# GpSimd makes the output weights' low half, new step lists for both ends, and a last tile whose feed-forward runs in halves

## The chip, the cores and the metric

The kernel runs on one core of a Trainium2 chip. The metric is device time in microseconds. A core has TensorE (PE) for matrix products, VectorE (DVE), ScalarE (ACT) and GpSimd (POOL) for elementwise work, and SyncE (SP), which here only issues DMAs. Each engine works through its own instruction list in order, and waits on semaphores for the others.

## What is computed

```
q  = layernorm(layernorm(x)) @ Wq,  q = q*(1+scale) + shift     # 32 batches of 112 rows, 256 wide, 16 heads of 64
kv = layernorm(ctx) @ Wkv                                       # 32 batches of 375 keys
x  = x + tanh(g_x) * (softmax(q k^T / 8) v @ Wout)
h  = gelu(bitlinear(layernorm(x), W1, b1))                      # 256 -> 1024
x  = x + tanh(g_f) * bitlinear(h, W2, b2)                       # 1024 -> 256
bitlinear(x, W, b): rms-normalise each row, scale by 127/max|row|, round and clip to int8;
                    W ternary (-1, 0, 1) by its mean absolute value; product, rescaled, plus b
```

## The kernel before

Attention goes batch by batch, 0 to 31. Products are made in three float16 matmuls (high times high, high times low, low times high), so each weight and each intermediate is split into a high half (`_h`, made by ACT) and a low half (`_l`, the rest after subtraction, mostly made by DVE). The feed-forward goes by token tiles 0 to 27 of 128 rows; one tile becomes ready after about each batch.

No loop order is left to chance: for each engine there are written lists of named steps. `ORDER` is the steady part, `FIRST` what runs in its place at the start (batches 0 and 1), and `LAST` what runs at the end (batches 30 and 31 and the last tiles). A pair like `("K3", 1)` is step K3 of batch 1. For the steps of tiles, `sequence` turns the number b into tile b - b//8 - 1, so 31, 30, 29, 28, 27 in the lists are the tiles 27, 26, 25, 24, 23. In this document the tile number is given.

The steps that matter here, in the order in which a batch or a tile meets them:
- LNA (POOL) and LNW (ACT): scales and normalised context `ctx_n`, `x_n`, from the statistics BA, BB, BS (DVE). Z0, Z1, ZX (PE): their transposes. ZF, ZXF (ACT), ZS, ZXS (POOL): evacuation and split.
- K0 to K7, V00 to V12, Q0, Q1 (PE): projections, each in one of three PSUM banks (`work`), evacuated by KH or VH (ACT), then KL or VL (DVE); for Q by QF (ACT) and QS (POOL). A bank is given to the jobs in turn, so a job waits for the evacuation of the third job before it.
- S0 to S7 (PE): scores of a pair of heads; M (DVE) the maxima, E (ACT) the exponentials, PH (ACT or DVE) the high half of the probabilities, PL (POOL) the low half, T (SP) the DMA transpose, A0 to A7 (PE) the product with v, N (DVE) the division. S of pair p waits for E of pair p-2, and E of pair p waits for PL of pair p-2.
- OO0, OO1 (PE) with OH (ACT), OT (DVE): transposed attention output. WO (PE): output projection of a tile. X1, XST, SC1 (DVE), RM1, XQ, XB (POOL), XR (ACT): residual, statistics, quantisation of the tile. XT (PE), XTE (DVE): its transpose. F0, F1 (PE), HE0, HE1 (DVE): first linear layer in two halves of 512 columns. GE, SQ, HR (ACT): gelu, sum of squares, rounding. HMX, SC2 (DVE), RM2, HQ (POOL): maximum, scales, quantised hidden row. HT (PE), HTE (DVE): its transpose. F2 (PE), YE (DVE), ST (SP): second layer, output row, store. Up to tile 25 the two transposes are DMA transposes issued by SP (XD, HD); for tiles 26 and 27 (`TAIL = 2`) PE does them.
- At the start the weights come in by DMA and are split: WKH0, WKH1, WQH, WVH, WOH (ACT, `wkv_h` and so on), WKL0, WKL1, WQL, WVL, WOL (DVE). AS0, AS1 (DVE) sum the absolute feed-forward weights.

The line numbers in the profile: 448 PL, 473 and 475 LNA, 510 HQ, 521 the ACT weight splits, 598 and 599 LNW, 608 E, 629 GE, 632 SQ, 637 HR, 650 the DVE weight splits, 662 AS, 805 HTE of the last tiles, 814 HTE of the others, 820 HE, 824 HMX, 718 to 725 the scales, 832 YE, 844 to 846 the three matmuls of a product, 863 S, 918 Z, 946 HT, 965 F2.

Of the kernel before, what the change touches and what calls it, by code (L numbers as in the profile page):

```python
# [1007 lines left out]
```

## Time and profile before

| | us |
|---|---|
| median of 3 runs | 1119.22 (1117.04 to 1120.62) |
| the profiled execution, its own time | 1121.15 |
| its span | 1119.3 |
| PE busy in the span | 1068.0 (95%) |
| ACT busy | 970.7 (87%) |
| DVE busy | 946.4 (85%) |
| POOL busy | 772.1 (69%) |

The busy times say which engine is nearly full; the 40 slices of the page say where it is not, and the chain that ended last says what the end of the span waited for. Waits, the timeline and the stretches then show which instruction ended an idle time.

### The profile page before, as it was taken

The numbers are of one execution on the slowest core, as the hardware profiler recorded it, in microseconds if no ns is written. First come the engines' busy times: TensorE is split into PE (matmuls) and PEld (weight loads), VectorE is DVE, ScalarE is ACT, GpSimd is POOL, SyncE is SP. The second block draws the span as 40 slices with busy tenths as digits, with TensorE's granted clock in tenths as the row PEclk, the third lists the DMA queues.
The fourth block names the chain that finished last, engine by engine and source line by source line (L and its number), as shares of the span: only waits on it lengthen the run. The fifth ranks groups of instructions, "written<-read, shape, count | busy, mean of one in ns | idle before, by whom it ended". The sixth has DMA issues, their size and how long they took to land.

```text
span 1119.3 us, 32134 instructions
## 1 busy us (share of the span) xinstructions
PE 1068.0 (95%) x11910; PEld 733.5 (66%) x11910; DVE 946.4 (85%) x2112; ACT 970.7 (87%) x1865; POOL 772.1 (69%) x837
## 2 busy tenths in 40 slices
...
PEclk9899999999999999999999999999999999999996
...
GB/s 272 86 109 107 101 106 122 123 97 126 115 114 118 133 104 101 123 115 110 134 119 99 120 118 99 122 127 104 115 119 120 109 137 112 97 124 106 112 114 24
DMA packets 408153, 129.08 MB, mean 115 GB/s; under 512 B 389792, under 2 KB 402848, under 8 KB 408000
## 3 DMA queue, kind: packets, MB, share of 16 engines
...
## 4 chain that ended last, share of the span: by engine, by line
PE 78%; ACT 9%; DMA 5%; issue 3%; DVE 2%; POOL 1%; POOLq 0%; DVEq 0%; SPq 0%; ACTq 0%
PE work L844 16%; PE work L846 16%; PE work L845 16%; PE ps_s L863 11%; DMA pt<-pn 4%; PE ps_o L844 3%; PE ps_o L846 3%; PE ps_o L845 3%; PE work L927 3%; ACT prob L608 2%; ACT q_f L574 2%; ACT L608 2%; PE work L956 2%; PE work L918 2%; PE work L965 2%
## 5 line engine op out<-in xcount | busy, mean ns | idle before, releaser
L448 POOL TENSOR_TENSOR pn<-prob,pn 112x750 f16<-112x750 f32 x256 | 400.2, 1569 | 117.5 <-ACT pn L618 97.8
L608 ACT ACTIVATE prob<-ps_s,neg_max 112x375 f32<-112x375 f32 x512 | 265.1, 573 | 10.5 <-DVE neg_max L759 7.5
L759 DVE TENSOR_REDUCE neg_max<-ps_s 112x2 f32<-112x750 f32 x256 | 237.6, 929 | 21.6 <-PE ps_s L863 21.5
L844 PE MATMUL ps_o<-v_h,pt 128*128 128x65 f16 (+1 forms) x1536 | 166.5, 194 | 9.1 <-DMA pt<-pn 7.6
L844 PE MATMUL work<-z,wkv_h 128*128 128x375 f16 x512 | 168.4, 329 | 2.7 <-POOL z L469 2.5
L681 DVE SCALAR_TENSOR_TENSOR k_l<-work,k_h 128x375 f16<-128x375 f32 x256 | 136.4, 541 | 38.4 <-ACT k_h L530 38.3
L530 ACT ACTIVATE k_h<-work 128x375 f16<-128x375 f32 x256 | 121.4, 488 | 53.4 <-PE work L846 48.6
L846 PE MATMUL work<-z,wkv_l 128*128 128x375 f16 x512 | 167.2, 327 | 0.0
L845 PE MATMUL work<-z,wkv_h 128*128 128x375 f16 x512 | 166.8, 326 | 0.0
L845 PE MATMUL ps_o<-v_l,pt 128*128 128x65 f16 (+1 forms) x1536 | 166.3, 192 | 0.0
L846 PE MATMUL ps_o<-v_h,pt 128*128 128x65 f16 (+1 forms) x1536 | 166.3, 193 | 0.0
L844 PEld LDWEIGHTS ps_o<-v_h,pt 128*128 128x128 f16 (+1 forms) x1536 | 143.4, 97 | 22.5 <-DMA pt<-pn 10.4
L845 PEld LDWEIGHTS ps_o<-v_l,pt 128*128 128x128 f16 (+1 forms) x1536 | 142.6, 98 | 9.5
L844 PE MATMUL work<-wkv_h,z 128*128 128x512 f16 (+1 forms) x384 | 146.8, 382 | 1.2 <-DVE k_l L681 1.2
L846 PE MATMUL work<-wkv_h,z 128*128 128x512 f16 (+1 forms) x384 | 145.5, 379 | 0.0
L845 PE MATMUL work<-wkv_l,z 128*128 128x512 f16 (+1 forms) x384 | 145.4, 379 | 0.0
L846 PEld LDWEIGHTS ps_o<-v_h,pt 128*128 128x128 f16 (+1 forms) x1536 | 142.5, 97 | 0.0
L681 DVE SCALAR_TENSOR_TENSOR v_l<-work,v_h 128x512 f16<-128x512 f32 (+1 forms) x192 | 128.3, 681 | 7.1 <-ACT v_h L530 6.6
L530 ACT ACTIVATE v_h<-work 128x512 f16<-128x512 f32 (+1 forms) x192 | 115.3, 601 | 11.4 <-PE work L846 9.5
L618 ACT ACTIVATE pn<-prob 112x750 f16<-112x750 f32 x128 | 107.8, 842 | 0.1
L574 ACT ACTIVATE q_f<-work,side_add,side_mul 128x112 f32<-128x112 f32 x256 | 93.9, 466 | 2.9 <-PE work L846 2.8
L863 PE MATMUL ps_s<-k_h,q_h 64*112 64x375 f16 x512 | 88.7, 343 | 2.2 <-ACT prob L608 1.8
(135 smaller groups left out, 2723.5 us busy)
## 6 DMA issues: line engine op xcount, KB each, us to landing
...
pt<-pn SPq DMA_TRANSPOSE x256, 3.5
...
stage<-in_wkv SPq DMA_DIRECT2D x2, 1024.0 KB, 9.3
stage<-in_w SPq DMA_DIRECT2D x2, 1024.0 KB, 13.1
stage<-in_wq SPq DMA_DIRECT2D x1, 1024.0 KB, 8.2
```

The source lines that it names most:

```text
L448: g.tensor_tensor(buf[:, 1, :, 0:SK], prob[:, p % 2], buf[:, 0, :, 0:SK], ALU.subtract).then_inc(p_lo, 1)
L530: a.activation(dst, src, ACT.Identity, scale=1.0 / W_SCALE).then_inc(hi_done, 1)
L574: i = a.activation(q_f[:, c, :], work[:, BANK[job], m * SQ:(m + 1) * SQ], ACT.Identity, bias=add, scale=mul)
L608: i = a.activation(prob[:, p % 2, h, :], ps_s[0:SQ, 2 * (p % 2) + h, 0:SK], ACT.Exp, bias=neg_max[:, 2 * (p % 2) + h:2 * (p % 2) + h + 1])
L618: a.activation(pn[g % PBUF][:, 0, :, 0:SK], prob[:, p % 2], ACT.Identity).then_inc(p_hi_act, 1)
L681: v.scalar_tensor_tensor(out=dst, in0=src, scalar=1.0 / W_SCALE, in1=hi_part, op0=ALU.mult, op1=ALU.subtract).then_inc(evacuated[BANK[job] ...
L759: v.tensor_reduce(neg_max[:, 2 * (p % 2):2 * (p % 2) + 2], ps_s[0:SQ, 2 * (p % 2):2 * (p % 2) + 2, 0:SK], X, ALU.max, negate=True).then_in ...
L844: t_.matmul(dst, sh, mh, start=(n == 0), stop=False)
L845: t_.matmul(dst, sh, ml, start=False, stop=False)
L846: i = t_.matmul(dst, sl, mh, start=False, stop=(n == len(pairs) - 1))
L863: i = t_.matmul(ps_s[0:SQ, 2 * (p % 2) + h, 0:SK], q[r, p, :], k[r, p, :], start=(n == 0), stop=(n == 2))
L927: i = t_.transpose(w[:, m * SQ:(m + 1) * SQ], attn[:, c * P:(c + 1) * P], ident[0:SQ, 0:SQ])
```

## The change

Five things are changed.
1. The step WOL (low half of the output weights) goes from DVE's list, where it was two SCALAR_TENSOR_TENSOR of 128x1024, to POOL's, where it is one TENSOR_SCALAR and one TENSOR_TENSOR of 128x2048, ahead of PL0 of batch 0.
2. All `FIRST` and `LAST` lists are new orders of the same steps. `ORDER` is as it was.
3. WO waits for the second half of the attention output (OO1) only ahead of its fifth of eight column blocks, rather than ahead of the first.
4. For the last tile (27) GE, HR, HQ, HT, HTE and F2 run in two halves of 512 columns; the first half of HT goes to a free bank of `ps_s`.
5. `deq2t`, the output scale, has two columns, one for even and one for odd tiles.

```diff
 FIRST["ACT"]
-    ("LNW", 0), ("WKH0", 0), ("ZF1", 0), ("ZF0", 0), ("WQH", 0), ("WKH1", 0), ("KH1", 0), ("WVH", 0),
-    ("KH0", 0), ("KH2", 0), ("ZXF", 0), ("WOH", 0), ("KH4", 0), ("KH3", 0), ("LNW", 1), ("QF0", 0),
+    ("WKH0", 0), ("LNW", 0), ("WKH1", 0), ("ZF1", 0), ("ZF0", 0), ("WQH", 0), ("KH0", 0), ("ZXF", 0),
+    ("WVH", 0), ("KH1", 0), ("KH2", 0), ("KH3", 0), ("LNW", 1), ("KH4", 0), ("QF0", 0), ("ZF0", 1),
+    ("KH5", 0), ("KH7", 0), ("ZF1", 1), ("WOH", 0), ("KH6", 0), ("VH02", 0), ("E0", 0), ("KH0", 1),
 FIRST["PE"]
-    ("Z1", 0), ("Z0", 0), ("K1", 0), ("K0", 0), ("K2", 0), ("ZX", 0), ("K4", 0), ("K3", 0),
-    ("Q0", 0), ("Z0", 1), ("K7", 0), ("K5", 0), ("K6", 0), ("Z1", 1), ("S0", 0), ("S1", 0),
+    ("Z1", 0), ("Z0", 0), ("ZX", 0), ("K0", 0), ("K2", 0), ("K1", 0), ("K3", 0), ("K4", 0),
+    ("Q0", 0), ("Z0", 1), ("K5", 0), ("K7", 0), ("Z1", 1), ("S0", 0), ("K6", 0), ("V02", 0),
 FIRST["DVE"]
-    ("BA", 0), ("BB", 0), ("BS", 0), ("WKL0", 0), ("ZS1", 0), ("WQL", 0), ("WKL1", 0), ("KL1", 0),
-    ("BA", 1), ("KL0", 0), ("BB", 1), ("KL2", 0), ("BS", 1), ("WVL", 0), ("KL4", 0), ("KL3", 0),
-    ("WOL", 0), ("KL7", 0), ("KL5", 0), ("AS0", 0), ...
+    ("BA", 0), ("BB", 0), ("BS", 0), ("WKL0", 0), ("WKL1", 0), ("ZS1", 0), ("WQL", 0), ("BA", 1),
+    ("KL0", 0), ("BB", 1), ("BS", 1), ("KL1", 0), ("KL2", 0), ("WVL", 0), ("KL3", 0), ("KL4", 0),
+    ("AS0", 0), ("KL5", 0), ("KL7", 0), ...
 FIRST["POOL"]
+    ("LNA", 0), ("ZS0", 0), ("SD", 0), ("ZXS", 0), ("LNA", 1), ("QS0", 0), ("ZS0", 1), ("ZS1", 1),
+    ("WOL", 0), ("PL0", 0), ("QS1", 0), ("PL1", 0), ("PL2", 0), ("LNA", 2), ("PL3", 0), ("ZXS", 1),
 LAST["PE"], its end
-    ("A2", 31), ("A3", 31), ("WO", 30), ("F2", 28), ("A4", 31), ("A5", 31), ("A6", 31), ("A7", 31),
-    ("XT", 30), ("OO0", 31), ("OO1", 31), ("F0", 30), ("F1", 30), ("WO", 31), ("F2", 29), ("XT", 31),
-    ("F1", 31), ("F0", 31), ("HT", 30), ("F2", 30), ("HT", 31), ("F2", 31),
+    ("S6", 31), ("S7", 31), ("OO1", 30), ("V10", 31), ("F0", 29), ("A2", 31), ("V12", 31), ("A3", 31),
+    ("F1", 29), ("WO", 30), ("A4", 31), ("A5", 31), ("F2", 27), ("OO0", 31), ("A6", 31), ("A7", 31),
+    ("OO1", 31), ("XT", 30), ("F1", 30), ("WO", 31), ("F0", 30), ("F2", 28), ("XT", 31), ("F0", 31),
+    ("F1", 31), ("F2", 29), ("HT", 30), ("F2", 30), ("HT", 31), ("F2", 31),
 LAST["ACT"], its end
-    ("OH0", 31), ("OH1", 31), ("HR", 29), ("GE", 30), ("SQ", 30), ("XR", 31), ("HR", 30), ("GE", 31),
+    ("XR", 30), ("OH1", 31), ("HR", 29), ("GE", 30), ("XR", 31), ("SQ", 30), ("HR", 30), ("GE", 31),
     ("SQ", 31), ("HR", 31),
 LAST["DVE"], its end
-    ("N3", 31), ("XTE", 30), ("SC2", 29), ("OT0", 31), ("OT1", 31), ("HE1", 30), ("HE0", 30), ("X1", 31),
-    ("XST", 31), ("HTE", 29), ("SC1", 31), ("HMX", 30), ("YE", 29), ("XTE", 31), ("SC2", 30), ("HE1", 31),
-    ("HE0", 31), ("HTE", 30), ("YE", 30), ("HMX", 31), ("SC2", 31), ("HTE", 31), ("YE", 31),
+    ("X1", 30), ("XST", 30), ("YE", 27), ("N2", 31), ("OT0", 31), ("SC1", 30), ("N3", 31), ("HMX", 29),
+    ("XTE", 30), ("OT1", 31), ("HTE", 28), ("SC2", 29), ("HE1", 30), ("X1", 31), ("XST", 31), ("HE0", 30),
+    ("SC1", 31), ("YE", 28), ("HMX", 30), ("XTE", 31), ("HTE", 29), ("SC2", 30), ("HE1", 31), ("HE0", 31),
+    ("YE", 29), ("HMX", 31), ("HTE", 30), ("SC2", 31), ("YE", 30), ("HTE", 31), ("YE", 31),
 LAST["POOL"], its end
-    ("PL5", 31), ("XB", 29), ("PL6", 31), ("PL7", 31), ("RM1", 30), ("RM2", 29), ("XQ", 30), ("HQ", 29),
-    ("XB", 30), ("XB", 31), ("RM1", 31), ("RM2", 30), ("XQ", 31), ("HQ", 30), ("RM2", 31), ("HQ", 31),
+    ("PL5", 31), ("HQ", 28), ("PL6", 31), ("PL7", 31), ("RM1", 30), ("XB", 30), ("XQ", 30), ("RM2", 29),
+    ("HQ", 29), ("RM1", 31), ("XQ", 31), ("RM2", 30), ("HQ", 30), ("RM2", 31), ("XB", 31), ("HQ", 31),
 LAST["SP"], its end
-    ("RS", 30), ("T1", 31), ("T2", 31), ("ST", 27), ("XD", 29), ("HD", 28), ("T3", 31), ("T4", 31),
-    ("T5", 31), ("T6", 31), ("T7", 31), ("ST", 28), ("RS", 31), ("HD", 29), ("ST", 29), ("ST", 30),
+    ("T1", 31), ("XD", 29), ("T2", 31), ("T3", 31), ("T4", 31), ("RS", 30), ("T5", 31), ("T6", 31),
+    ("T7", 31), ("RS", 31), ("ST", 27), ("HD", 28), ("HD", 29), ("ST", 28), ("ST", 29), ("ST", 30),
     ("ST", 31),
...
+            def split_output_weights():                       # POOL
+                pool.wait_ge(hi_split[3], 1)
+                g.tensor_scalar(wout_f, wout_f, W_SCALE, 0.0, ALU.mult, ALU.add)
+                pool.drain()
+                g.tensor_tensor(wout_l[:], wout_f, wout_h[:], ALU.subtract).then_inc(lo_split[3], 1)
...
+                        for half in LAST_HALVES:               # GE of the last tile, ACT; LAST_HALVES is [1, 0]
+                            act.wait_ge(evacuated[BANK[f"F{half}", b]], USE[f"F{half}", b])
+                            c = slice(half * HALF, (half + 1) * HALF)
+                            a.activation(hid_g[:, c], hid[:, c], ACT.Gelu).then_inc(gelu_done, 1)
...
+                if name == "HT" and b == NT - 1:               # PE
+                    pe.wait_ge(exp_done, B * PAIRS)
+                    pe.wait_ge(hq_ready, b + 1)
+                    for c in range(4):
+                        i = t_.transpose(ps_s[:, 0, :].bitcast(F16)[:, c * P:(c + 1) * P], hid_q[:, c * P:(c + 1) * P], ident_h[:])
+                    i.then_inc(half_turned, 1)
+                    pe.wait_ge(hq_ready, b + 2)
+                    for c in range(4):
+                        i = t_.transpose(wh[:, c * P:(c + 1) * P], hid_q[:, (c + 4) * P:(c + 5) * P], ident_h[:])
```

## Rows read from the trace of the kernel before

**Rows 1.** The page: busy share, TensorE's granted clock in 40 slices.
```profile
PE 1068.0 (95%) x11910; PEld 733.5 (66%) x11910; DVE 946.4 (85%) x2112; ACT 970.7 (87%) x1865; POOL 772.1 (69%) x837
...
PEclk9899999999999999999999999999999999999996
```

**Rows 2.** Waits of PE over the span: total us, times, longest.
```profile
PE work L918 <- ACT x_n L599: 17.0, 2, 13.3
```

**Rows 3.** Stretches: length, busy us (instructions) PE, PEld, DVE, ACT, POOL, granted clock, DMA, GB/s.
```profile
75.00:1040.00 965.00, 953.29 (x10795) 659.61 (x10794) 836.27 (x1882) 870.63 (x1692) 700.19 (x734) 1.00 0.67 115
...
34.00:35.00 1.00, 1.00 (x5) 0.48 (x4) 0.24 (x1) 0.00 (x0) 0.00 (x0) 0.50 0.32 129
...
36.00:37.00 1.00, 1.00 (x10) 0.72 (x10) 1.00 (x2) 0.15 (x1) 0.00 (x0) 1.00 0.00 0
...
1084.00:1086.00 2.00, 0.99 (x33) 0.89 (x30) 1.68 (x7) 0.00 (x0) 1.21 (x3) 1.00 0.65 114
...
1098.00:1100.00 2.00, 1.13 (x6) 0.35 (x4) 1.74 (x4) 0.55 (x1) 0.41 (x1) 0.50 0.00 0
```

**Rows 4.** Timeline of ACT at the start: start us, us, instruction, [idle before, releaser].
```profile
13.07 1.04 ACT L521 ACTIVATE wkv_h<-stage 128x1024 f16<-128x1024 f32 x1
...
25.64 1.91 ACT L521 ACTIVATE wout_h<-stage 128x2048 f16<-128x2048 f32 x1 [1.66 <-DMA stage<-in_wout]
...
28.19 1.57 ACT L598 ACTIVATE ctx_n<-ctx_in,ln_nb,ln_rs 125x256 f32<-125x256 f32 x3
```

**Rows 5.** Timeline of PE at the start: Z0 of batch 1, first scores.
```profile
30.40 0.86 PE L918 MATMUL work<-ident,ctx_n 125*128 125x125 f32 x3 [3.74 <-ACT x_n L599]
...
36.74 0.37 PE L863 MATMUL ps_s<-k_h,q_h 64*112 64x375 f16 x2
```

**Rows 6.** DMA issues from 1.5 to 1.9 us: first half of wkv, us to landing.
```profile
stage<-in_wkv SPq DMA_DIRECT2D x1, 1024.0 KB, 8.7
```

**Rows 7.** Timeline of DVE at the start: WVL.
```profile
24.66 2.73 DVE L650 SCALAR_TENSOR_TENSOR wkv_l<-stage,wkv_h 128x1024 f16<-128x1024 f32 x2
```

**Rows 8.** Timeline of POOL at the start: LNA of batches 1 and 2, PL0.
```profile
25.13 2.02 POOL L473 TENSOR_TENSOR ln_rs<-ln_ve,minus_half 125x4 f32<-125x4 f32 x1
...
42.25 1.56 POOL L448 TENSOR_TENSOR pn<-prob,pn 112x750 f16<-112x750 f32 x1 [1.64 <-ACT pn L618]
...
49.95 1.02 POOL L473 TENSOR_TENSOR ln_rs<-ln_ve,minus_half 125x4 f32<-125x4 f32 x1 [0.23 <-DVE ln_ve L702]
```

**Rows 9.** Timeline of PE at the end: last attention product, then HT and F2 of tile 27.
```profile
1087.16 0.20 PE L844 MATMUL ps_o<-v_h,pt 128*128 128x65 f16 x1 [0.75 <-DMA pt<-pn]
...
1112.50 1.01 PE L946 MATMUL work<-ident_h,stage 128*128 128x128 f16 x8 [5.30 <-POOL stage L510]
1114.39 1.86 PE L965 MATMUL work<-w_t,stage 128*128 128x256 f16 x8 [0.88 <-DVE stage L805]
```

**Rows 10.** Timeline of DVE at the end: XTE, HTE, YE, HMX.
```profile
1099.60 0.29 DVE L801 TENSOR_SCALAR xqt<-work 128x256 f16<-128x256 f16 x1 [0.16 <-PE work L942]
...
1104.50 0.69 DVE L805 TENSOR_SCALAR stage<-work 128x1024 f16<-128x1024 f16 x1 [1.81 <-PE work L946]
1107.34 0.48 DVE L832 SCALAR_TENSOR_TENSOR y<-work,deq2t,stage 128x256 f32<-128x256 f32 x1 [2.15 <-PE work L965]
1107.74 1.21 DVE L824 TENSOR_REDUCE amax<-stage 128x1 f32<-128x1024 f32 x1
```

**Rows 11.** Timeline of ACT at the end: GE and HR of tile 27.
```profile
1102.72 1.06 ACT L629 ACTIVATE stage<-stage 128x1024 f32<-128x1024 f32 x1 [0.55 <-DVE stage L820]
...
1109.98 1.24 ACT L637 ACTIVATE stage<-stage,round_col,qs 128x1024 f32<-128x1024 f32 x1 [5.02 <-DVE qs L725]
```

**Rows 12.** Timeline of POOL at the end: HQ of tile 24, RM2 and HQ of tile 27.
```profile
1070.45 1.05 POOL L510 TENSOR_SCALAR stage<-stage 128x1024 f16<-128x1024 f32 x1 [3.75 <-ACT stage L637]
...
1105.38 0.54 POOL L507 TENSOR_TENSOR g_rs<-g_ve,minus_half 128x1 f32<-128x1 f32 x1
...
1111.31 1.05 POOL L510 TENSOR_SCALAR stage<-stage 128x1024 f16<-128x1024 f32 x1 [5.39 <-ACT stage L637]
```

More of the change, by code:

```diff
@@ L224 @@
     BANK[job], USE[job] = n % WORK_BANKS, n // WORK_BANKS + 1
+GELU_COUNT = [t + 1 if t < NT - 1 else t + 2 for t in range(NT)]
+LAST_HALVES = [int(s[0][2]) for s in sequence("DVE") if s[0] in ("HE0", "HE1") and s[1] == NT - 1]
 HI_COUNT = {s: n + 1 for n, s in enumerate(s for s in sequence("ACT") if s[0][0:2] in ("KH", "VH"))}
@@ L294, in build @@
         ssq, g_ve, g_rs = (sb(n, [P, 1]) for n in ("ssq", "g_ve", "g_rs"))
-        amax2, clip2, inv2, qs2, deq2, deq2t = (sb(n, [P, 1]) for n in ("amax2", "clip2", "inv2", "qs2", "deq2", "deq2t"))
+        amax2, clip2, inv2, qs2, deq2 = (sb(n, [P, 1]) for n in ("amax2", "clip2", "inv2", "qs2", "deq2"))
+        deq2t = sb("deq2t", [P, 2])
         xqt_r, hqt_r = sb("xqt_r", [P, KC, P], F16), sb("hqt_r", [P, FF // P, P], F16)
@@ L509, in step @@
                     pool.wait_ge(scaled2, b + 1)
-                    g.tensor_scalar(hid_q[:], hid_r[:], -ROUND, 1.0, ALU.add, ALU.mult).then_inc(hq_ready, 1)
+                    if b < NT - 1:
+                        g.tensor_scalar(hid_q[:], hid_r[:], -ROUND, 1.0, ALU.add, ALU.mult).then_inc(hq_ready, 1)
+                    else:
+                        for half in range(2):
+                            pool.wait_ge(scaled2, b + 1 + half)
+                            c = slice(half * HALF, (half + 1) * HALF)
+                            g.tensor_scalar(hid_q[:, c], hid_r[:, c], -ROUND, 1.0, ALU.add, ALU.mult).then_inc(hq_ready, 1)
             for name, b in sequence("POOL"):
@@ L624, in step @@
                         act.wait_ge(tern_ready[1], 1)
-                    for half in range(2):
-                        act.wait_ge(evacuated[BANK[f"F{half}", b]], USE[f"F{half}", b])
                     if b > 0:
                         act.wait_ge(scaled2, b)
-                    a.activation(hid_g[:], hid[:], ACT.Gelu).then_inc(gelu_done, 1)
+                    if b < NT - 1:
+                        for half in range(2):
+                            act.wait_ge(evacuated[BANK[f"F{half}", b]], USE[f"F{half}", b])
+                        a.activation(hid_g[:], hid[:], ACT.Gelu).then_inc(gelu_done, 1)
+                    else:
+                        for half in LAST_HALVES:
+                            act.wait_ge(evacuated[BANK[f"F{half}", b]], USE[f"F{half}", b])
+                            c = slice(half * HALF, (half + 1) * HALF)
+                            a.activation(hid_g[:, c], hid[:, c], ACT.Gelu).then_inc(gelu_done, 1)
                 if name == "SQ":
-                    act.wait_ge(gelu_done, b + 1)
+                    act.wait_ge(gelu_done, GELU_COUNT[b])
                     a.activation(hid[:], hid_g[:], ACT.Square, accum_out=ssq[:]).then_inc(hid_sq, 1)
@@ L636, in step @@
                         act.wait_ge(hq_ready, b)
-                    a.activation(hid_r[:], hid_g[:], ACT.Identity, bias=round_col[:],
-                                 scale=qs2[:]).then_inc(scaled2, 1)
+                    if b < NT - 1:
+                        a.activation(hid_r[:], hid_g[:], ACT.Identity, bias=round_col[:], scale=qs2[:]).then_inc(scaled2, 1)
+                    else:
+                        for half in range(2):
+                            c = slice(half * HALF, (half + 1) * HALF)
+                            a.activation(hid_r[:, c], hid_g[:, c], ACT.Identity, bias=round_col[:], scale=qs2[:]).then_inc(scaled2, 1)
             for name, b in sequence("ACT"):
@@ L831, in step @@
                     dve.wait_ge(full[BANK["F2", b]], USE["F2", b])
-                    v.scalar_tensor_tensor(out=y[:], in0=work[:, BANK["F2", b], 0:D], scalar=deq2t[:], in1=x1_b2[:, b % 4, :],
+                    v.scalar_tensor_tensor(out=y[:], in0=work[:, BANK["F2", b], 0:D], scalar=deq2t[:, b % 2:b % 2 + 1], in1=x1_b2[:, b % 4, :],
                                            op0=ALU.mult, op1=ALU.add).then_inc(evacuated[BANK["F2", b]], 1)
```

40 lines of the change are left out of this document (28 added, 12 removed), and 135 rows, old and new, of the table CAST_ACT.

## Prediction

> **What bounds the kernel now.** I read four views, in this order. The busy times and the slices of the page come first: PE is busy for 95% of the span, and every slice but the first and the last few is full [rows 1]. The stretches say the same of the middle: from 75 to 1040 us PE is busy for 953.29 of 965 us at full clock [rows 3]. `ORDER`, which runs there, isn't changed, so nothing can be won or lost in the middle, and what the start wins stays won at the end. The waits of PE come next: the largest is 17.0 us, two waits of Z for `x_n` [rows 2], the load at 0 us (13.3) and one of 3.74 us at batch 1 [rows 5]. The timelines of the two ends say the rest. In the first 37 us and in the last 35 us PE idles, and behind the idle it runs at half clock (granted clock 0.50, the 1.2 GHz level) [rows 3]. So the change is two separate questions, one for each end, and their answers add.
>
> **The start, step by step.** Before, ACT runs into WOH while the output weights are still on their way: it idles 1.66 us, works 1.91 us, and only then comes LNW of batch 1, at 28.19 us [rows 4]. PE, out of other work, waits 3.74 us, starts Z0 at 30.40 [rows 5], and finds its clock halved: granted 0.50 in the stretch at 34 us, 1.00 again at 36 us [rows 3]. That is some 5.5 us at half rate, so 5.5 / 2 = 2.75 us lost beyond the wait.
> After, WOH stands behind ZF1 of batch 1, and BA, BB, BS of batch 1 stand ahead of KL1 and WVL. I follow it. K0 is done at about 19.4, KL0 at 21.1, BB and BS at 22.8; LNA takes 1.0 to 2.0 us [rows 8] and ends about 24.1; LNW, 2.06 us with `x_n` (1.57 of it in [rows 4]), ends about 26.2 instead of 30.25. Now something else is late: Z0 of batch 1 needs the bank of K3, and KL3 stands behind WVL, 2.73 us long [rows 7], from 24.15 to 26.9. Z0 so starts at about 27.4, and PE, with Q0 done at 26.4, idles 1.0 us. I take it that such a short idle leaves the clock up: before, it fell in one of 3.74 us [rows 5].
> - Wait for `x_n`: 3.74 to 1.0, a gain of 2.7.
> - Half clock from 30.4 to 36 gone: a gain of 2.7 (0 if the short idle costs the clock all the same).
> - WKH0 ahead of LNW of batch 0: its weights are issued at 1.55 and take 8.7 us [rows 6], so it can start at 10.25; at 1.04 us [rows 4] it holds LNW, which started at 11.09, till 11.25: a loss of 0.15. If the transfer came 1 us later, 1.15.
> - New small waits, of K1 for ZXF, K4 for KL2, K6 for KL5 behind AS0: a loss of 0.7 together (0 to 1.5).
> The start gains 2.7 + 2.7 - 0.15 - 0.7 = 4.6 us, between 1.5 and 6. Counted another way: the first scores, at 36.74 before [rows 5], start at about 30.1 with one K product of 1.0 us less behind them, a gain of 5.6 there, of which the wait of K6 takes 0.3 later.
>
> **The low half of the output weights on GpSimd.** DVE loses two instructions; PE waits for neither, so I book nothing for it. POOL gains two: TENSOR_SCALAR of 2048 columns, twice the 1024 of HQ at 1.05 [rows 12], is 2.1; TENSOR_TENSOR of 2048 by the 750 of PL at 1.56 [rows 8] is 2048/750 x 1.56 = 4.3 at most, 3.9 without the fixed part of each instruction. Together about 6.2 us, from WOH's end, 32.8, to 39.0. Queued behind it are PL0, QS1, PL1: PL0 ends at 40.6, QS1 at 42.3, and S4 of batch 0 needs it. By my count PE comes to S4 at 43.4, so there are about 1.1 us of cover and the cost is 0. Each us beyond the cover costs PE one. The dearest bound is in the row of LNA: 2.02 us at 25.13, while DVE runs WVL, against 1.02 for the same instruction at 49.95 [rows 7, 8]. Doubled, the split takes 12.4, and PE stands 5 us at S4; with the clock falling behind such a wait (2.7 again) that is 5 to 8.
> The Trainium skill bears on this (SBUF — State Buffer, "SBUF: two separate sides"): GpSimd and DVE share a port pair that is locked for a whole instruction, against DVE work in a two-port mode or with two operands in SBUF. It speaks against the move, and the doubled LNA agrees with it. By that rule only the casts of PH on DVE, at this place few and short, would hold the split up, by about an instruction each.
>
> **The end, step by step.** Its parts follow each other. First, the last attention. Before, POOL stands 3.75 us at HQ of tile 24 in front of PL3 [rows 12], the last pairs come late, and PE is busy for only 0.99 of the 2 us from 1084, then waits 0.75 us for the transpose of the last pair, at 1087.16 [rows 3, 9]. After, HQ of tile 24 stands behind PL5, S7 stands ahead of OO1, V10 and F0 (3.2 us of work), and F2 of tile 23 and OO0 fill in behind. PE has 0.4 us less to do up to A7. Against it stands N2 behind X1, XST and YE of the tiles 26 and 23, about 1.0 us of wait at A6. I book a gain of 1.8 us, between 0 and 3.
> Second, from A7 to XTE of the last tile (1099.60 [rows 10]), 12 us. Gains: OO0 is done ahead of it, WO doesn't wait whole for OO1, HTE of tile 25 leaves the chain (0.7 to 1). Losses: N3 stands behind SC1, HE0 of tile 26 stands in HTE's place, and XR of tile 27 stands behind GE of tile 26 (0.3 each). I book 0, between -1.5 and +1.
> Third, from there to the last scale. Before: GE of tile 27 ends at 1103.78 [rows 11], but its maximum HMX stands behind HTE and YE of tile 26 on DVE, and YE waits 2.15 us for F2 [rows 10]; HMX ends at 1108.95, HR starts at 1109.98 [rows 11]. After, HMX stands ahead of both. But DVE takes HE1 first and PE now makes F0 first, so HE1 waits for the second product: F0 and F1 are as many columns as F2, 1.86 us at half clock [rows 9], so 0.93 later, and the halved gelu gives 0.5 back. GE ends at 1104.2, YE of tile 25 at about 1104.3, HMX at 1105.5, HTE of tile 26 (0.69 [rows 10]) at 1106.2; the sum of squares comes by POOL at 1105.92 before [rows 12], 0.4 later now, 1106.35; the scales take 0.9. HR starts at 1107.3: a gain of 2.7, between 2 and 3.3.
> Fourth, the last tile in halves. Before, from HR to the end of F2: 1109.98 to 1116.25, 6.3 us, of HR 1.24, HQ 1.05, HT 1.01, HTE 0.69, F2 1.86 and hand-overs [rows 9 to 12]. After, a half each of HR (0.65), HQ (0.55), then HQ's second half ends 2.0 behind HR's start, HT's second 2.65, HTE's 3.15, and half of F2 is left, done at 4.45. A gain of 1.85, between 1.2 and 2.2. YE of tile 26 stands ahead of the first HTE half; F2 of tile 26 ends at 1108.1, and the half is needed at 1109.2, so it is covered by 0.6 us. YE of tile 27 also needs the store of tile 26, about 2 us after its YE; that leaves 1 us. The second column of `deq2t` costs nothing: the write is the same 128x1.
> The end gains 1.8 + 0 + 2.7 + 1.85 = 6.35 us, between 2 and 8.5.
>
> **The sum.** The profiled execution took 1121.15 us, its span 1119.3, 1.85 around it. 1121.15 - 4.6 - 6.35 = 1110.2. It was 1.93 us above the median of the runs, so the median after is 1119.22 - 10.95 = 1108.3 us.
>
> **The rivals.**
> - The split on GpSimd becomes the bound of the start. It takes 10 to 12 us, PL0, QS1 and PL1 are late, PE stands at S3 to S6 of batch 0. For it: the doubled LNA. Against it: the PL instructions run beside DVE all the time and take 1.56 [rows 8]. Time: 1108.3 + 5 = 1113 to 1116.
> - The end gains only by its last two parts: PE is no earlier at A7, because E7, PH7, PL7 and the transpose are one chain that a better order only shifts, and the second part loses its 1.5. Time: 1108.3 + 1.8 + 1.5 = 1111.6, to 1113 with the third part at its lower end.
> - The lists do not do what they say: new stalls at both ends give back what is won, for instance F2 of tiles 23 and 24, put off so far that PE has work where it needs none. Time: 1117 to 1121.
> - Slower: one mechanism, the same split at GpSimd, at three times my price. It starts at 32.8; the cover of 1.1 us and the 11 us of gain are used up when it takes 6.2 + 1.1 + 11 = 18.3 us, less 2.7 if the clock falls, so from about 15.6 us on the kernel is slower than before; at 20 us it would be about 1123.
>
> **How the numbers follow.** Chances: forecast, 1104 to 1111: 0.60. Split as bound, 1113 to 1116: 0.12. The end at its last parts only, 1111 to 1113: 0.16. Nothing won, 1117 to 1121: 0.08. Slower: 0.04. The predicted time is the first's, 1108.3. The range from 1103.8 to 1114.5 holds all of the first and third and most of the second: about 0.85. A measurement of this kernel can tell about 0.3%, 3.4 us, so faster is below 1115.9: 0.60 + 0.16 + 0.11 = 0.87; same takes the rest of the second and most of the fourth, 0.08; slower 0.05.
>
> **What would show it.** Right: PE's wait for `x_n` at batch 1 about 1 us or gone, first scores at 30 to 31 us, no stretch at granted clock 0.50 between 28 and 37; the two POOL instructions of the split at 2.1 and 4 us, PL0 starting about 39; no wait of PE for `q_l` or `prob` over 1 us before 55. At the end HMX of tile 27 ahead of HTE and YE of tile 26, HR about 1.2 us or less behind RM2, and 4.5 us from HR to the end of the last F2. Wrong: a new wait of several us at S4, a long wait for the transposes of tile 24 or 25, whose issue on SP now stands behind the store of tile 23, or A7 no earlier in respect of the end.

## The result, and the profile after

| us | before | after |
|---|---|---|
| median of all runs | 1119.93 (1117.04 to 1122.23) | 1118.14 (1112.96 to 1122.23) |
| profiled execution | 1121.15 | 1117.53 |
| its span | 1119.3 | 1115.4 |

The ratio is 0.9979 (95% interval 0.9970 to 0.9989): 1.8 us less, not the 10.95 that were forecast, and outside the range. The page after: the engines' busy times, then PE and its clock in 40 slices, as in [rows 1].

```profile
PE 1064.2 (95%) x11910; PEld 732.2 (66%) x11910; DVE 943.0 (85%) x2111; ACT 969.0 (87%) x1867; POOL 779.1 (70%) x840
...
PE   3888999999999999999999999999999999999995
...
PEclk9999999999999999999999999999999999999998
```

PE has about the same work. The half clock that [rows 3] had at 34 us is gone; the slices show no other loss. What is new is in the waits of PE after (columns: engine, tile, line, what ended it; us in total, times, longest). Lines of the kernel after: 452 PL, 479 the last instruction of LNA, 509 XQ, 528 HQ of the last tile, 617 `x_n` of LNW, 709 KL and VL, 718 N, 784 M, 802 BA, 877 to 879 the three matmuls, 896 S, 951 Z, 979 XT, 1015 F2; in the kernels of the experiments they differ by a few.

```profile
PE work L951 <- ACT x_n L617: 14.3, 2, 13.2
PE ps_o L877 <- DMA pt<-pn: 11.4, 8, 2.7
PE work L979 <- POOL xq L509: 4.4, 1, 4.4
PE work L877 <- DVE k_l L709: 4.1, 3, 2.7
...
PE ps_o L877 <- DVE attn L718: 2.0, 2, 1.2
PE ps_s L988 <- POOL stage L528: 1.9, 1, 1.9
```

The waits for `x_n` fell from the 17.0 of [rows 2] to 14.3. Those for the transposed probabilities (`pt<-pn`, steps T) and for `k_l` rose; the same two groups in the trace of before:

```profile
PE ps_o L844 <- DMA pt<-pn: 7.6, 8, 1.4
...
PE work L844 <- DVE k_l L681: 1.2, 1, 1.2
```

A fixed stretch hides where that cost lies: from 75 to 1040 us PE was busy for 953.29 us before [rows 3], and after for

```profile
75.00:1040.00 965.00, 953.16 (x10807) 661.26 (x10806) 830.54 (x1870) 866.11 (x1687) 696.76 (x730) 1.00 0.67 114
```

The same: the stretch loses 3.1 us of PE's work up to 140 us and has it back behind that, 2.1 of it from 1017 to 1040 us, where PE idles less under the new last lists. Cut finer it shows (first two rows before, the other two after; columns as in [rows 3], busy us of PE second):

```profile
40.00:75.00 35.00, 34.57 (x387) 22.14 (x386) 31.02 (x57) 32.97 (x68) 23.66 (x24) 1.00 0.58 99
75.00:140.00 65.00, 61.88 (x694) 41.04 (x694) 52.77 (x108) 50.61 (x108) 44.41 (x44) 1.00 0.62 105
```
```profile
40.00:75.00 35.00, 31.77 (x335) 19.55 (x331) 29.52 (x54) 29.68 (x61) 23.06 (x22) 1.00 0.53 95
75.00:140.00 65.00, 58.82 (x636) 39.97 (x636) 45.77 (x94) 45.43 (x96) 41.28 (x40) 0.95 0.57 95
```

PE loses 2.8 us of work in the first stretch, 3.1 in the second, and clock there. The surest reading is by steps. The table gives the start of a step in PE's timeline less the start of the same step before (found by counting PE's matmuls in the order of its list; us, minus is earlier), and the median of each kernel:

| kernel | S0 of batch 0 | S0, 3 | S0, 30 | last F2 | median (of before beside it) |
|---|---|---|---|---|---|
| the change | -6.05 | +6.92 | +6.01 | -2.87 | 1118.14 (1119.93) |
| start_only | -5.98 | +6.51 | +5.56 | +4.73 | 1126.93 (1120.02) |
| end_only | +0.02 | +0.86 | +0.51 | -8.12 | 1113.29 (1120.02) |
| later_stats | -4.29 | +5.23 | +4.04 | -4.81 | 1115.36 (1120.02) |
| old_sp | -5.79 | +4.62 | +5.90 | -2.75 | 1116.08 (1120.02) |
| stats_and_sp | -5.90 | +2.11 | +2.58 | -6.29 | 1113.80 (1120.35) |
| weights_later | -4.48 | +3.25 | +2.26 | -6.40 | 1114.37 (1119.86) |
| small_loads | -6.80 | -2.24 | -2.41 | -11.30 | 1109.74 (1119.86) |
| split_on_pool | -1.38 | +3.13 | +3.34 | -4.25 | 1116.81 (1120.35) |
| spliced_start | -2.26 | -1.39 | -1.22 | -9.87 | 1110.99 (1119.86) |
| spliced_dve | -4.30 | -3.59 | -3.41 | -12.00 | 1110.05 (1120.44) |
| spliced_best | -3.57 | -0.15 | +0.53 | -8.15 | 1111.28 (1120.44) |
| repaired_start | -6.27 | +1.73 | +2.14 | -6.71 | 1112.75 (1119.86) |
| end_lists | +0.13 | +1.28 | +0.63 | -6.22 | 1114.82 (1120.35) |
| halves_only | +0.06 | -0.83 | -1.63 | -4.03 | 1119.37 (1120.35) |
| small_loads_before | +0.12 | -1.94 | -2.16 | -3.00 | 1118.15 (1120.44) |

Each row is one profiled execution. Four kernels with exactly the start of before (before, end_only, end_lists, halves_only) differ by up to 2.1 us at the scores of batch 3, so differences below about 2 us in this table say little.

The change is 6 us ahead at the first scores, and 7 us behind at the scores of batch 3: 13 us are lost between, and `FIRST` reaches that far. The end then wins 8.9 of it back. Those 13 us can be added up from the stretch between the two scores, before and then after:

```profile
36.74:132.28 95.54, 92.00 (x997) 59.59 (x997) 80.38 (x154) 78.66 (x161) 65.35 (x66) 1.00 0.59 98
```
```profile
30.69:139.20 108.51, 96.42 (x1003) 62.49 (x1003) 80.16 (x156) 80.21 (x162) 72.22 (x67) 0.97 0.52 91
```

PE idles 12.1 us instead of 3.5, which is 8.5 of the 13. It is busy 4.4 us longer: 1.1 is K6 of batch 0, which stood ahead of the first scores before (so in equal work the change was 5 us ahead there), and some 3.3 is the clock of 0.97 over 108.5 us. Two places carry most of it. First, DVE and PE after, at 30 to 38 us:

```profile
30.69 0.99 DVE L709 SCALAR_TENSOR_TENSOR k_l<-work,k_h 128x375 f16<-128x375 f32 x2
35.98 0.75 DVE L802 BATCH_NORM_STATS2 ln_bn<-ctx_in 125x6 f32<-125x256 f32 x2 [4.30 <-DMA ctx_in<-in_ctx]
36.66 0.92 DVE L784 TENSOR_REDUCE neg_max<-ps_s 112x2 f32<-112x750 f32 x1
37.49 0.54 DVE L709 SCALAR_TENSOR_TENSOR k_l<-work,k_h 128x375 f16<-128x375 f32 x1
```
```profile
27.19 0.52 PE L951 MATMUL work<-ident,ctx_n 125*128 125x125 f32 x3 [1.07 <-ACT x_n L617]
...
30.69 0.37 PE L896 MATMUL ps_s<-k_h,q_h 64*112 64x375 f16 x2 [0.22 <-POOL q_l L460]
...
38.09 0.39 PE L877 MATMUL work<-wkv_h,z 128*128 128x512 f16 x1 [2.68 <-DVE k_l L709]
```

BA of batch 2 (L802) stands ahead of M0 and KL6 of batch 0 in DVE's new list and waits 4.30 us for its context. KL6 is late, and PE waits 2.68 us for it. Second, transposes that stand directly behind a context load on SP: PE's waits for them are 7.3 us in this stretch, and were 1.9 before. The one of pair 3 of batch 0, issued at 54.0, and for comparison pair 0, issued at 41.4 with no load ahead of it (both after; what waited, and the time to landing):

```profile
L371 SPq DMA_TRANSPOSE pt<-pn x1: 2220/2220/2220, 54.0 to 54.0; - x1
...
  PE ps_o L877: 2.0, 1
DMA to landing us min/median/max: 7.3/7.3/7.3
```
```profile
L371 SPq DMA_TRANSPOSE pt<-pn x1: 1474/1474/1474, 41.4 to 41.4; - x1
...
DMA to landing us min/median/max: 3.2/3.2/3.2
```

The same at batch 1 (pair 2: 7.1 us, PE waits 2.72) and batch 2 (pair 2: 8.9 us, PE waits 2.55). Pair 2 of batch 2 stood behind a context load before too, and took 6.9 us; the new list has put it behind two more loads. Behind those two PE also runs at reduced clock, after:

```profile
94.00:98.00 4.00, 4.00 (x42) 2.57 (x39) 0.21 (x2) 1.27 (x3) 1.86 (x3) 0.64 0.89 205
129.00:132.00 3.00, 3.00 (x45) 3.00 (x44) 0.39 (x1) 0.00 (x0) 0.30 (x1) 0.54 1.14 258
```

### The profile page after: what moved, and what is told of

It reads as the page before. It is cut to its first block, busy times and chain, and to the rows that moved or that the text cites. A ratio compares the mean times of both kernels' runs of the same rounds, so it can differ in the third digit from the quotient of the medians.

```text
span 1115.4 us, 32139 instructions
## 1 busy us (share of the span) xinstructions
PE 1064.2 (95%) x11910; PEld 732.2 (66%) x11910; DVE 943.0 (85%) x2111; ACT 969.0 (87%) x1867; POOL 779.1 (70%) x840
## 4 chain that ended last, share of the span: by engine, by line
PE 75%; ACT 8%; DMA 5%; issue 4%; POOL 3%; DVE 2%; POOLq 1%; DVEq 0%; SPq 0%; ACTq 0%
PE work L877 14%; PE work L879 13%; PE work L878 13%; PE ps_s L896 11%; DMA pt<-pn 5%; PE ps_o L877 3%; PE ps_o L879 3%; PE ps_o L878 3%; PE work L960 2%; ACT L626 2%; ACT q_f L592 2%; PE work L1002 2%; ACT prob L626 2%; PE work L973 2%; PE work L975 2%
## 5 line engine op out<-in xcount | busy, mean ns | idle before, releaser
L709 DVE SCALAR_TENSOR_TENSOR k_l<-work,k_h 128x375 f16<-128x375 f32 x256 | 136.2, 541 | 30.6 <-ACT k_h L548 30.4
```

The lines of the kernel that those rows point to most:

```text
L709: v.scalar_tensor_tensor(out=dst, in0=src, scalar=1.0 / W_SCALE, in1=hi_part, op0=ALU.mult, op1=ALU.subtract).then_inc(evacuated[BANK[job] ...
```

## The experiments

Ratios are to the kernel before run beside each, with their 95% interval.

**The two ends apart.** start_only: 1126.93 us, 1.0065 (1.0048 to 1.0081). end_only: 1113.29, 0.9944 (0.9932 to 0.9957).

```diff
 start_only, from before: FIRST of all five engines from the change, WOL moved from DVE to POOL
 end_only, from the change: FIRST of all five engines from before, WOL on DVE
```

> The kernel before with only the start of the change: all FIRST lists of after, WOL on GpSimd. Theory: slower than before by 5 to 8 us, about 1126, with BA of batch 2 waiting about 4 us for its context and S0 of batch 3 some 7 us later than before. Rival (start not to blame): within 2 us of before. My prediction was 4.6 us faster.

> The changed kernel with its start as before: all FIRST lists of before, WOL on DVE. Theory: the two ends are separate, the start loses some 6 us and the end gains some 10 (in the two profiles S0 of batch 30 is 6.0 us later after, and the span still 3.9 shorter). So this kernel is 8 to 11 us faster than before, about 1110. Rival: the start of one profiled execution is not typical, both ends matter little, and this kernel is 1 to 3 us faster, like the whole change.

The start costs 6.9 us, the end gains 6.7. The spans add up (+4.4 and -8.4 against the -3.9 of the change); the medians add up to +0.2, 2 us from the -1.8 measured; each of the three has an interval of 1 to 2 us to either side, and the rest is left open.

**Repairs of the start.** Each takes one suspected wait out of the change.

```diff
 later_stats, FIRST["DVE"]
-("AS0", 0), ("KL5", 0), ("KL7", 0), ("BA", 2), ("M0", 0), ("KL6", 0), ("VL02", 0), ("M1", 0), ("KL0", 1), ("VL00", 0), ("BB", 2)
+("AS0", 0), ("KL5", 0), ("KL7", 0), ("M0", 0), ("KL6", 0), ("VL02", 0), ("M1", 0), ("KL0", 1), ("VL00", 0), ("BA", 2), ("BB", 2)
 old_sp, FIRST["SP"] (the list of before)
-("LD", 3), ("LX", 3), ("T3", 0), ("T4", 0), ("T5", 0)
+("T3", 0), ("LD", 3), ("T4", 0), ("LX", 3), ("T5", 0)
...
 weights_later
-                sp.dma_start(w2_f, ...); sp.dma_start(b1_row[:], ...)      # in load_late_weights
+                if b == 2: the same two                                    # at the end of load_queries
```

> The changed kernel with one step moved in FIRST of DVE: BA of batch 2 from ahead of M0 to ahead of BB of batch 2. Theory (DVE, standing 4.3 us for the context in front of M0, sets the first exponential back): E0 starts at about 34 instead of 37.6, PE's wait of 2.7 us for KL6 goes, and the kernel is 2 to 4 us faster than after if nothing else is late next. Rival (the transposes behind the loads are the cause): the wait goes, the gain is lost again at A3 of batch 0 and A2 of batch 1, and the time is within 1 us of after.

> The changed kernel with only SP's FIRST list of before, so that T3 of batch 0 is issued ahead of the context of batch 3, and T2 of batch 2 isn't behind three loads. Theory (loads ahead of transposes are the second cause): T3 of batch 0 lands in 3 to 4 us instead of 7.3, T2 of batch 2 in 7 instead of 8.9, the waits of PE of 2.0 and 2.6 us go or shrink, and the kernel is 2 to 4 us faster than after. Rival (the transposes are slow because the context load runs beside them wherever it stands): PE's waits move to another pair, and the time stays within 1 us.

> The change with both repairs of the start: BA of batch 2 behind M0 and M1 on DVE, and the first SP list of before (transposes ahead of the loads they stood behind). Each alone won 2 to 2.8 us over the change. Theory (two separate waits, both in the bound): they add up, 4 to 5 us less than the change, about 1113.5 us. Rival (the start is short of work for PE in these stretches whatever the order, a repaired wait comes back as the next one): no more than the better of the two, 1115 to 1116 us.

> The change, with the loads of w2 and b1 (1.5 MB) issued after the context and queries of batch 2 instead of ahead of them. Theory (BA of batch 2 waits 4.3 us because its context stands behind those weights in the DMA queues): the context lands at about 31 to 32 us instead of 36, BA waits for nothing, PE's 2.7 us for KL6 are gone, and the kernel takes 2 to 3 us less than the change, about 1115.5. Rival (the loads share the engines and none is first): it still lands at 35, within 1 us of the change.

later_stats: 1115.36, 0.9961 (0.9947 to 0.9976); PE no longer waits for KL6. old_sp: 1116.08, 0.9969 (0.9957 to 0.9981). Its T3 lands in 3.1 to 3.2 us, but T4, now the first behind the load, in 6.1, and PE waits 1.3 us for that one (pairs 2 and 3 first, then pair 4, of old_sp):

```profile
L371 SPq DMA_TRANSPOSE pt<-pn x2: 1306/1320/1335, 51.4 to 54.9; - x2
...
DMA to landing us min/median/max: 3.1/3.1/3.2
```
```profile
L371 SPq DMA_TRANSPOSE pt<-pn x1: 2029/2029/2029, 57.6 to 57.6; - x1
...
  PE ps_o L877: 1.3, 1
DMA to landing us min/median/max: 6.1/6.1/6.1
```

At batch 1 the wait only moved, from pair 2 (2.72 us) to pair 3 (8.3 us to land, PE waits 2.4); pair 2 of batch 2 still took 8.2 us, not the 7 expected, and PE's wait for it fell from 2.55 to 1.0. So the list decides which pair is hit, and a pair with more slack is hit more cheaply. stats_and_sp: 1113.80, 0.9935 (0.9919 to 0.9951), 4.3 us under the change, where the two alone gave 2.8 and 2.1: they nearly add. weights_later: 1114.37, 0.9954 (0.9942 to 0.9967), 3.8 us under the change, but for a reason only half the expected one. The statistics of batch 2 still start at 34.95 (35.98 in the change), not at 31 to 32: from the issue of the context (28.65, 27.07 in the change) it took 6.3 us instead of 8.9. The weights cost the context up to 2.6 us (it was also issued 1.6 later), and something else holds it as well. PE's wait for KL6 is down to 0.07, while its wait for `x_n` rose to 2.2, as it did in later_stats, where no load was moved (the cause is below). From the first scores to those of batch 3 PE idles 8.4 us instead of 12.1 (2.6 less for KL6, 1.1 less for the transposes) and is busy 1.5 less, at a clock of 0.98; the first scores come 1.6 later. That makes the 3.7 us that the two rows of the table differ by at batch 3.

repaired_start adds to stats_and_sp the later weights and an earlier ZS0 of batch 2 on GpSimd:

> The change with four repairs: BA of batch 2 behind M0 and M1, the first SP list of before, w2 and b1 loaded after the inputs of batch 2, and on GpSimd ZS0 of batch 2 ahead of PL6 as before. Theory (waits add): the first two gave 4.3 us, the others at most 0.3 and 0.8 more, 1112.7 to 1113.5 us. Rival (the last two only move waits on): 1113.8 or more.

1112.75, 0.9934 (0.9922 to 0.9946). The median lies in the theory's band, but the ratio is that of stats_and_sp, so nothing that can be measured came of the last two. PE's wait for T4 of batch 0 grew from 2.9 to 3.5 us.

**The loads themselves.** Both kernels leave out two thirds of three contexts, so their times only price the loads.

```diff
 small_loads (from the change) and small_loads_before (from before), in load_context
+                    if b in (3, 4, 5):
+                        sp.dma_start(ctx_in[:, 0:1, :], ctx[b].rearrange("(p t) d -> p t d", p=TP)[:, 0:1, :]).then_inc(ctx_loaded, 16)
```

> The change, but the context loads of batches 3, 4 and 5 bring only the first of every partition's three rows (a third of 375 KB); those batches' keys are not the reference's, all instructions are the same. Theory (the transposes are late because the load ahead of them holds the DMA engines): T3 of batch 0, T2 of batch 1 and T2 of batch 2 land in 3 to 4.5 us instead of 7.3, 7.1 and 8.9, PE's waits for them (2.04, 2.72, 2.55) shrink to under 0.5 each, and the kernel takes 4 to 6 us less than the change, about 1113. Rival (their lateness comes from their issue on SP or from the pairs themselves): they take as long as before, and the time is that of the change, 1118.

> The kernel before with the same cut: the context loads of batches 3, 4 and 5 bring a third of their rows (their keys are not the reference's). Theory (the kernel before hides nearly all of that contention, the new order exposes it): only its waits at A3 of batches 1 and 2 (1.40 and 0.52) go, 1.5 to 2.5 us less than before, 1117.5 to 1118.5, against 8.4 us in the change. Rival (the loads cost both kernels alike, and the loss of the change has another cause): 5 us or more.

small_loads: 1109.74, 0.9907 (0.9894 to 0.9920), 8.4 us under the change. The three transposes land in 4.4, 4.5 and 5.9 us instead of 7.3, 7.1 and 8.9; for the first:

```profile
L374 SPq DMA_TRANSPOSE pt<-pn x1: 1478/1478/1478, 55.1 to 55.1; - x1
...
DMA to landing us min/median/max: 4.4/4.4/4.4
```
```profile
75.00:100.00 25.00, 23.99 (x264) 14.89 (x261) 19.86 (x40) 19.88 (x42) 21.04 (x20) 1.00 0.52 107
```

PE's waits for them are 0, 0.11 and 0, and the clock is 1.00 from 75 to 100 us (second fence; 0.93 in the change). By the table this start is 9.2 us ahead of the change's at batch 3: the waits in between are 6.7 us shorter, PE's busy time 1.7, and 0.75 was there at the first scores, ahead of any of the cut loads. The same cut in the kernel before gives 2.3 us: 1118.15, 0.9977 (0.9968 to 0.9986). So both kernels have the contention; the old order hides 5 to 6 us more of it.

**The split on GpSimd.**

```diff
 split_on_pool, from end_only
-FIRST["DVE"]:  ("KL3", 0), ("WOL", 0), ("KL7", 0)        FIRST["POOL"]: ("ZS0", 1), ("PL0", 0)
+FIRST["DVE"]:  ("KL3", 0), ("KL7", 0)                    FIRST["POOL"]: ("ZS0", 1), ("WOL", 0), ("PL0", 0)
```

> The end-only kernel, with the low half of the output weights made by GpSimd directly ahead of PL0 of batch 0, and DVE without it; the start is otherwise that of before. Theory (the split costs nothing only where the rest of the start makes room): GpSimd ends ZS0 of batch 1 at 40.6, PL0 moves from 42.2 to about 46.8, and PE waits at S4: 3 to 4.5 us slower than the end-only kernel, 1116.5 to 1118. Rival (DVE's gain and PE's other work cover it): within 1 us of the end-only kernel, 1113 to 1114.

1116.81, 0.9972 (0.9961 to 0.9983): 3.5 us slower than end_only, as the theory says. In split_on_pool GpSimd is still at it at 45 us, and PE waits 2.1 us for `q_l` and 1.3 for `v_l` (waits between 40 and 55 us):

```profile
41.22 4.07 POOL L485 TENSOR_TENSOR wout_l<-stage,wout_h 128x2048 f16<-128x2048 f32 x1
```
```profile
PE ps_s L896 <- POOL q_l L460: 2.1, 1, 2.1
PE work L877 <- DVE v_l L709: 1.3, 1, 1.3
```

The second of these waits is DVE's, and it comes from GpSimd as well. DVE's first PH, ahead of the maxima and of that VL, took 3.15 us beside the split, and 0.54 in end_only (split_on_pool, then end_only):

```profile
42.55 3.15 DVE L791 CAST pn<-prob 112x750 f16<-112x750 f32 x1
```
```profile
43.85 0.54 DVE L786 CAST pn<-prob 112x750 f16<-112x750 f32 x1
```

It ended at 45.70, 0.4 us behind the split (45.29).

**What of the start can be kept.** spliced_start takes every engine's new list up to the last evacuation ahead of the first scores, then the old one, and the old SP list whole. spliced_dve is the same with WOL on DVE behind KL6. spliced_best is spliced_start with three small moves.

```diff
 spliced_start, FIRST["PE"] (the other engines alike)
 ("Q0", 0), ("Z0", 1), ("K5", 0), ("K7", 0), ("Z1", 1),
-("S0", 0), ("K6", 0), ("V02", 0), ("S1", 0), ("K0", 1), ("V00", 0), ("Q1", 0), ("K1", 1), ("S2", 0)
+("K6", 0), ("S0", 0), ("S1", 0), ("V02", 0), ("V00", 0), ("K0", 1), ("Q1", 0), ("S2", 0)
...
 spliced_dve, FIRST
-POOL: ("ZS1", 1), ("WOL", 0), ("PL0", 0)
+DVE:  ("KL6", 0), ("WOL", 0), ("M0", 0)
 spliced_best: w2 and b1 as in weights_later; ACT ("KH6", 0), ("WOH", 0); POOL ("QS1", 0), ("PL1", 0)
```

> The change up to the first scores on every engine (with the split on GpSimd), and from there the first lists of before, SP's whole list too; the end is that of the change. Theory (what the start won up to the first scores was given back by the order behind them): about 5 us of the 6 are kept at the scores of batch 3, less the wait of the transposes at batch 1 (1 to 2): 1108 to 1110 us. Rival (the work behind the first scores is bound by DVE, GpSimd and the DMAs, whatever the order): the gain at the scores of batch 3 is under 1 us, 1112.5 to 1113.5, as with the start of before.

> The spliced start, with the low half of the output weights made by DVE again (2.35 us, behind KL6 of batch 0) and taken from GpSimd. Theory (where the high half comes late, DVE has no hole for the low half, and GpSimd's hole costs less): M0 is 2 us later, PL0 no longer waits for the split; PE's 1.27 us at S4 turns into about 2 at the second pair of value products or S2; 0.5 to 1.5 us slower than the spliced start, about 1112. Rival (the move to GpSimd is worth nothing): 1111 or less.

> The spliced start with w2 and b1 loaded after the inputs of batch 2, WOH behind KH6 of batch 0 on ACT, and QS1 ahead of PL1 of batch 0 on GpSimd. Theory (three small waits in the bound: 0.6 us of K6, 1.27 us at S4, and what the late weights hold up): 1 to 2 us less than the spliced start, about 1109.5 us. Rival (each only moves a wait on): 1111, the same.

spliced_start: 1110.99, 0.9914 (0.9898 to 0.9930), 2.3 us under end_only and the first that keeps a gain at both ends with all its work done. spliced_dve: 1110.05, 0.9911 (0.9897 to 0.9924), the same or better: DVE has room for the low half in the new start as in the old (spliced_dve, behind an idle 2 us):

```profile
33.77 0.55 DVE L701 SCALAR_TENSOR_TENSOR k_l<-work,k_h 128x375 f16<-128x375 f32 x1 [1.99 <-ACT k_h L540]
34.23 2.35 DVE L670 SCALAR_TENSOR_TENSOR wout_l<-stage,wout_h 128x1024 f16<-128x1024 f32 x2
```

The theory falls; moving the split is worth nothing that can be measured. spliced_best: 1111.28, 0.9921 (0.9909 to 0.9934), no gain: with QS1 ahead of PL1 the wait at S4 fell from 1.27 to 0.60, and A1 of batch 0 waited 2.0 us for its transpose instead. Here too the first PH fell beside the split, from 40.13, and took 2.04 us. A part of the scatter between these kernels isn't in the lists: the wait of PE for `x_n` of batch 1 was 1.07 in spliced_dve and 2.21 in spliced_start and spliced_best, with the same steps ahead of it. The traces show where it comes from. `x_n` waits for the last instruction of LNA, `ln_nb`, a 125x4 one on GpSimd, and that one can fall beside WVL on DVE, two instructions that each read two operands from SBUF (small_loads, spliced_dve, spliced_start, and DVE in the last):

```profile
23.97 0.20 POOL L482 TENSOR_TENSOR ln_nb<-ln_nm,ln_rs 125x4 f32<-125x4 f32 x1
```
```profile
24.25 1.02 POOL L479 TENSOR_TENSOR ln_nb<-ln_nm,ln_rs 125x4 f32<-125x4 f32 x1
```
```profile
24.41 1.98 POOL L479 TENSOR_TENSOR ln_nb<-ln_nm,ln_rs 125x4 f32<-125x4 f32 x1
```
```profile
23.98 2.35 DVE L678 SCALAR_TENSOR_TENSOR wkv_l<-stage,wkv_h 128x1024 f16<-128x1024 f32 x2
```

Started just ahead of WVL it took 0.20 us. Started beside WVL's first instruction it ended within 0.1 us of the end of that one (1.02) or of the second (1.98). All eleven kernels with the new start fall into these three groups: 0.20, and `x_n` was in time, PE waiting 0.41 to 0.45 for the bank of K3; 0.88 to 1.14, and it waited 1.07 for `x_n` (the change is here); 1.98, and it waited 2.20 or 2.21. In the table it is the first column: -4.3 and -4.5 in the two kernels with PE's whole new list where it took 1.98, -5.8 to -6.8 in the other six. How often each case happens over all runs isn't recorded.

**The end in two.**

```diff
 end_lists: before with LAST of the change and deq2t[P, 2]
 halves_only: before with the halves of tile 27, the split wait of WO and deq2t[P, 2]; FIRST and LAST of before
```

> The kernel before with the last lists of the change and the output scale in two columns, and nothing else: no halves in the last tile, no split wait of the last WO product. Theory (the gain of the end comes mostly from the order of the last lists, less than 2 us from the halves): about 1.9 to 2.4 us over the end-only kernel, 1115 to 1116 us; the start of the last F2 of tile 27 about 5.5 to 6 us earlier than before. Rival (the halves carry the end): 1118 us or more.

> The kernel before, all its lists kept, with only the last tile's feed-forward in halves, the WO product waiting for its second half midway, and the output scale in two columns. Theory: HR of the last tile to the end of its last F2 takes 4.45 us instead of 6.3, so about 1.5 to 2 us less than before, 1118 us. If halves and lists were independent, the two kernels' gains add up to that of the end-only one (6.7 us). Rival: the second half's hand-overs eat it up, within 0.5 us of before.

end_lists: 1114.82, 0.9955 (0.9944 to 0.9967), 5.5 us under before. halves_only: 1119.37, 0.9991 (0.9982 to 0.9999), 1.0 us. Together 6.5, and end_only has 6.7: they add. The lists are most of the end.

## Why the prediction was wrong, point by point

**The start up to the first scores: the time right, in part by luck.** Z0 of batch 1 at 27.19 after a wait of 1.07 (27.4 and 1.0 were worked out), first scores at 30.69 (30.1), granted clock 1.00 from 15 to 40 us, where [rows 3] had 0.50 at 34. But Z0 was to wait for the bank of K3 behind WVL. WVL ran earlier, from 23.66 to 26.02 (24.15 to 26.9), and KL3 was done at 26.47; what Z0 waited for was `x_n`, done at 27.05 and not at 26.2, because `ln_nb` took 0.88 us beside WVL. In small_loads, where it took 0.20, Z0 did wait for that bank, and for 0.45. The small waits, 0.7 in the sum and 1.5 at most, came to 1.7: 1.12 of K4 for KL2, 0.35 of K5, 0.22 for `q_l`. In equal work the start was 5 us ahead at the first scores, 4.6 booked.

**The split: sizes right, cost nought as said.** After:

```profile
33.47 1.90 POOL L483 TENSOR_SCALAR stage<-stage 128x2048 f32<-128x2048 f32 x1
35.52 4.07 POOL L485 TENSOR_TENSOR wout_l<-stage,wout_h 128x2048 f16<-128x2048 f32 x1
39.82 1.56 POOL L452 TENSOR_TENSOR pn<-prob,pn 112x750 f16<-112x750 f32 x1 [0.23 <-ACT pn L636]
```

6.1 us against 6.2; PL0 waited 0.23 us for ACT, not for the split. The rule of the shared port pair (the Trainium skill, SBUF — State Buffer, "SBUF: two separate sides") had no visible effect on the split, and the doubling of [rows 8] didn't come: DVE stood in its wait up to 35.98, its first PH started at 44.82, after the split had ended at 39.6, and took 0.54. In split_on_pool, where DVE worked beside it, the second instruction took the same 4.07, but here the other side paid: PH took 3.15 us. I had expected PH to hold the split up, and it was the other way round; the traces agree with the rule in that the one that started later was late. The doubled LNA of [rows 8] fits the same rule, and so do the three lengths of `ln_nb` above. With the old start `ln_rs` fell beside WVL, 2.01 to 2.02 us in five kernels and 3.08 in end_only, where PE waited 4.40 us for `x_n` instead of 3.38 to 3.87; with the new start it stood ahead of WVL and took 1.03 in all eleven. For LNA I had allowed up to 2.0 us and worked on with an end at 24.1; it came at 24.94.

**The step that failed** is in the first part: "`ORDER`, which runs there, isn't changed, so nothing can be won or lost in the middle, and what the start wins stays won at the end", and with it the second count of the start, which stopped at the first scores at 36.74. The first lists run on for another hundred us, to the scores of batch 3, and 13 us were lost there. I had followed the new order for the 13 steps of PE that lie ahead of the first scores and not for the others. Even the lower end of the start's gain, 1.5, left out a loss. Measured, the start is +6.9 where -4.6 was booked, 11.5 us apart. That is more than the whole miss of 9.2; the end gave 0.35 more than booked, and the other 2.0 are those by which the two ends don't add up. Two checks in the diff would have pointed at it: BA of batch 2 moved ahead of M0 and KL6 (in the trace of before the load next to its context, issued at 30.6, took 5.5 us), and T3 of batch 0 and T2 of batch 1 moved directly behind a load, T2 of batch 2 behind two more. I had named the second kind as a danger only at the end, for tiles 24 and 25. Every sign that was to show the prediction right came (the last below), and none of those that were to show it wrong: not one of them looked between 55 us and the last tiles.

**The end: right, 6.35 booked, 6.7 measured**, but not by its parts. In end_only's trace, from the S0 of batch 30:
- Last attention: 1.8 booked (0 to 3), 4.4 measured (+0.51 at S0 of batch 30, -3.91 at A7 of batch 31). I had looked at the lists from 1084 us; they begin at 1017. PE's busy time from 1017 to 1087 us, before, and then after:

```profile
1017.00:1087.00 70.00, 64.22 (x786) 44.29 (x783) 61.34 (x126) 56.61 (x107) 46.34 (x47) 1.00 0.55 115
```
```profile
1017.00:1087.00 70.00, 69.01 (x833) 48.51 (x832) 61.03 (x125) 60.49 (x111) 48.94 (x48) 1.00 0.61 118
```
- A7 to the transpose of the last tile: 0 booked, -3.91 became -4.03: 0.1.
- To the last scale: 2.7 booked. HR starts at 1103.27 in end_only, 6.71 ahead of [rows 11], of which 4.03 was there already: 2.7.
- Halves: 1.85 booked (1.2 to 2.2). From HR's start to F2's end 6.3 before, in end_only 1103.27 to 1108.14 = 4.87 (rows below): 1.4; by the medians of halves_only 1.0. In the change it took 3.97 (4.5 was the sign): its F2 took 1.17 us instead of 1.87, at a granted clock of 0.83 from 1111.5 to 1112.7, against 0.50 in end_only.

```profile
1103.27 1.52 ACT L658 ACTIVATE stage<-stage,round_col,qs 128x512 f32<-128x512 f32 x2 [2.02 <-DVE qs L745]
1106.27 1.87 PE L1010 MATMUL work<-w_t,stage 128*128 128x256 f16 x8
```

HMX stood ahead of HTE and YE of tile 26 as said, in the change at 1105.57, HTE at 1106.69, HR at 1108.72.

The parts make 8.6 in this trace and 6.7 in the medians; the profiled execution of before was itself 1.2 us above its median, that of end_only 0.6 below. So the close agreement of 6.35 with 6.7 owes something to luck: in the trace the first part alone gave 2.6 more than booked.

**The rivals.** "Nothing won: new stalls give back what is won", 1117 to 1121, came true with a chance of 0.08, at one end only and by waits I hadn't looked for. The rival of the split named the right place, but not for this kernel, and not by a longer split: in split_on_pool the split took no longer, came too late, and cost 3.5 us. The slower case was set up on the split alone; start_only, at 1126.93 us, shows that the order of the first lists can do it.
